# A gated state-space block rewritten: one-pass products on stacked parts, two norms side by side, silus in fours, sums on GpSimd

## The reference

```python
xn = layernorm(x) * norm_w + norm_b
p = xn @ w_in.T;  x1, x2 = p[:C], p[C:]
u = x1 @ ssm_in_w.T
xss, z = silu(u[:C]), silu(u[C:])
xd = einsum(xss, x_proj_w)             # per direction: dtr (R), B (S), C (S)
dt = softplus(einsum(dtr, dt_w) + dt_b)
bc = sum(B * C over S)
y = xss * sum over directions (bc * dt + Ds)
y = (layernorm(y) * out_norm_w + out_norm_b) * z
x = x + ((y @ ssm_out_w.T) * silu(x2)) @ w_out.T
```

## Time and profile before

| | us |
|---|---|
| median of 3 runs (lowest, highest) | 5749.59 (5741.32, 5757.34) |
| span of the profiled execution | 5743.1 |
| the gated block in it: first DMA issue to last write of X | 0.75 to 702.80 |
| first product on x | 35.63 |

### The profile page before, as it was taken

One profiled execution on the slowest core, in us unless ns is written; L12 is line 12 of the kernel. 1 busy time (PEld: TensorE's weight loads), 2 busy tenths in 40 slices (PEclk: granted clock), 3 DMA queues, 4 the chain that ended last, 5 costly groups with the idle time before them and its releaser, 6 DMA issues. The chain is left out here.

```text
span 5743.1 us, 74310 instructions
## 1 busy us (share of the span) xinstructions
PE 4971.3 (87%) x16018; PEld 2207.8 (38%) x16018; DVE 4640.4 (81%) x5047; ACT 2949.7 (51%) x4576; POOL 3832.2 (67%) x2568
## 2 busy tenths in 40 slices
PE   6999889897779999998297888888888888888887
PEld 1222256464256666665152222222222222222222
DVE  4876643434418989899797999999999999999996
ACT  5776544443311111111135777777777777777776
POOL 0000032322418898888786999989998999999993
PEclk9998899998889999998698999999999999999998
DMA  2000000001777787776405667667766666677663
GB/s 47 0 0 0 7 1 1 0 1 56 226 158 139 138 152 140 147 141 107 91 9 138 185 183 189 185 182 189 187 186 178 186 185 187 184 189 189 187 184 100
DMA packets 373418, 711.24 MB, mean 124 GB/s; under 512 B 76604, under 2 KB 111224, under 8 KB 358936
## 3 DMA queue, kind: packets, MB, share of 16 engines
q1 hardware_dynamic: 373144, 708.17, 50.2%
HBM read 575.33 MB, written 82.32 MB: 115 GB/s over the span
## 5 line engine op out<-in xcount | busy, mean ns | idle before, releaser
L2015 POOL TENSOR_TENSOR l_hc<-l_h,l_c_rep 128x512 f32<-128x512 f32 x1536 | 1929.8, 1276 | 216.0 <-DVE l_h L2069 187.1
L2069 DVE TENSOR_TENSOR_SCAN l_h<-l_p_da,l_h,l_bu 128x512 f32<-128x512 f32 x1120 | 1412.8, 1279 | 10.5 <-ACT l_p_da L1920 8.8
L1920 ACT ACTIVATE l_p_da<-l_p_da,l_a_neg 128x512 f32<-128x512 f32 x1536 | 1008.5, 658 | 733.8 <-PE l_p_da L1775 712.9
L1221 POOL TENSOR_TENSOR l2b_prod<-l2b_v,l2b_attn 128x1568 f32<-128x1568 f32 x276 | 937.3, 3461 | 242.9 <-DVE l2b_osum L1269 125.2
L1775 PE MATMUL l_p_da<-l_stacked,l_pick 96*128 96x512 f32 x1536 | 908.9, 593 | 191.3 <-DVE l_h L2069 179.1
L2054 DVE TENSOR_TENSOR l_bu<-l_du_rep,l_p_b 128x512 f32<-128x512 f32 x1280 | 855.7, 669 | 29.7 <-DMA l_du_rep<-du_scratch 22.5
L1775 PEld LDWEIGHTS l_p_da<-l_stacked,l_pick 96*128 96x128 f32 x1536 | 293.7, 192 | 1162.4 <-DVE l_h L2069 900.3
L1269 DVE TENSOR_REDUCE l2b_osum<-l2b_prod 128x32 f32<-128x1568 f32 x384 | 665.7, 1780 | 62.9 <-POOL l2b_prod L1221 59.2
L1783 PE MATMUL l_p_y<-l_hc,l_y_pick 128*32 128x512 f32 x3072 | 566.4, 626 | 74.3 <-POOL l_hc L2015 71.7
L1174 ACT ACTIVATE l2b_logits<-l2b_conv,l2b_this_b 98x512 f32<-98x512 f32 x96 | 66.2, 689 | 870.5 <-PE l2b_conv L1139 870.5
L615 POOL TENSOR_TENSOR l_w_pos_low<-l1a_w_sed,l_w_pos_high 96x1536 fp32r<-96x1536 f32 x1 | 4.1, 4123 | 711.2 <-DVE l_w_fc_high L595 711.2
(11 more groups left out here) (267 smaller groups left out, 8905.2 us busy)
## 6 DMA issues: line engine op xcount, KB each, us to landing
l_du_rep<-du_scratch SPq DMA_DIRECT2D x1536, 256.0 KB, 3.8
l2b_img_high<-qkv_scratch SPq DMA_DIRECT2D x192, 306.2 KB, 5.6
l2b_img_low<-qkv_scratch SPq DMA_DIRECT2D x192, 306.2 KB, 9.4
l_stacked<-l_parts SPq DMA_DIRECT2D x512, 96.0 KB, 2.7
l2b_v<-v_scratch SPq DMA_DIRECT2D x192, 152.0 KB, 6.4
qkv_scratch<-l2a_strip SPq DMA_DIRECT2D x32, 840.0 KB, 5.2
du_scratch<-l_du SPq DMA_DIRECT2D x128, 192.0 KB, 2.1
v_scratch<-l2a_v_strip SPq DMA_DIRECT2D x32, 228.0 KB, 4.2
```

The source lines that it names most:

```text
L1221: return eng.tensor_tensor(dst.rearrange("q x (dy dx) -> q x dy dx", dx=WIN), window, attn_half[:, :, unit % 2].rearrange("q x (dy dx) -> ...
L1920: act.activation(p_da[i % DAS][:], p_da[i % DAS][:], ACT.Exp, scale=a_neg[:, k * G + GRP[i]:k * G + GRP[i] + 1]).then_inc(s_da, 1)
L2015: pool.tensor_tensor(hc[:, (G * par + i) % HCS, :], h[:, i, :], c_rep[:, par, :], ALU.mult).then_inc(s_hc, 1)
L2069: dve.tensor_tensor_scan(h[:, i, way], p_da[i % DAS][:, way], of, state, ALU.mult, ALU.add).then_inc(s_h, 1)
```

## The change

The gated block is rewritten; the other blocks are the same.

- Part of the products becomes one-pass. The weights are no longer multiplied together: one product with `w_bcd` (128 columns) gives the rank parts of all directions twice, b and c. ScalarE copies the two rank parts rounded to float32r, VectorE writes what the rounding left (`rank_low`), and the stack of 96 rows, high, high and low, is the operand of four products with a `w_dt` whose rows are stacked as well (high, low, high). For b*c the stack is high, low and zero rows (`bc_high`, `bc_low`), against `pick`.
- The first norm of tile t+6 and the second norm of tile t-2 lie side by side in two neighbouring banks, and square, Ln, Exp and the product with the inverse deviation work on 1024 elements, where both parts exist.
- The projections and silus of four tiles are taken together, before step t where t is 4g-2 (`project`, `silus`). Tiles are kept in eight slots instead of four. The first centering behind such a group waits for all its silus (`centered`).
- abs is taken from PSUM with the bias on ScalarE, max(.,0) with the bias on VectorE; GpSimd adds the two (`add_log`), adds the directions (`add_gains`, `whole_sum`) and applies the scale and shift of both norms (`affine`).
- The loop is written out, TensorE waits for one quarter of x at a time, and the DMAs are as many as before; the weights of delta and pick are larger (96 x 384 each).

```diff
@@ gated_ssm_block @@
+    GROUP, SLOTS = 4, 8
+    KR, KS = K * R, K * S
...
-        w_bc = sb("l0_w_bc", [C, 2, K * S])
-        xp_dt = sb("l0_xp_dt", [R, K, C])
-        dt_w = sb("l0_dt_w", [R, K, C])
-        w_dt = sb("l0_w_dt", [C, K, C])
-        pick = sb("l0_pick", [K * S, K, C])
+        w_bcd = sb("l0_w_bcd", [C, 128])
+        w_dt = sb("l0_w_dt", [3 * KR, K, C], F32R)
+        pick = sb("l0_pick", [3 * KS, K, C], F32R)
...
+        a = sb("l0_a", [C, SLOTS, N])
+        z = sb("l0_z", [C, SLOTS, N])
+        sg = sb("l0_sg", [C, SLOTS, N])
+        sq = sb("l0_sq", [C, 2, N])
+        rstd = sb("l0_rstd", [C, 2, N])
+        nrm = sb("l0_nrm", [C, 2, N])
+        yz = sb("l0_yz", [C, N])
+        sgated = sb("l0_sgated", [C, N])
+        split = sb("l0_split", [3 * KR, 2, N], F32R)
+        bs = sb("l0_bs", [128, N])
+        bcp = sb("l0_bcp", [KS, N])
+        bc_split = sb("l0_bc_split", [3 * KS, 2, N], F32R)
+        log_part = sb("l0_log_part", [C, K, N])
...
+        half_sum = sb("l0_half_sum", [C, 2, N])
+        whole_sum = sb("l0_whole_sum", [C, 2, N])
...
+        banks = ctx.enter_context(nc.psum_tensor("l0_p", [128, 8, N], F32))
+        p_c, p_v = banks[0:C, 0:2, :], banks[0:C, 2:4, :]
+        p_s, p_o = banks[0:C, 2, :], banks[0:C, 3, :]
+        p_in = [[banks[0:C, i, :] for i in which] for which in ((0, 1, 2), (3, 4, 5))]
+        p_dt = [banks[0:C, 4 + i, :] for i in range(2)]
+        p_bcd, p_bc = banks[:, 6, :], banks[0:C, 7, :]
...
+        def parts_of(n):
+
+            return slice(0 if n >= SLOTS else 1, 2 if n < TILES else 1)
+
+        def all_steps(step, silu_group):
+
+            for t in range(-2, TILES + 2):
+                if t % GROUP == GROUP - 2 and t + 2 < TILES:
+                    silu_group((t + 2) // GROUP)
+                step(t, t >= 0 and t < TILES, t + 1 >= 0 and t + 1 < TILES, t + 2 < TILES, t >= 2)
...
+            def centered(n):
+                if n >= GROUP and n % GROUP == 0 and n <= TILES:
+                    pe.wait_ge(s_silu, n)
+                elif n:
+                    pe.wait_ge(s_nrm, n)
+                if n >= SLOTS:
+                    pe.wait_ge(s_y, n - SLOTS + 1)
+                    mm = pe.matmul(p_c[:, 0, :], center[:], a[:, n % SLOTS, :], start=True, stop=True)
+                if n < TILES:
+                    pe.wait_ge(s_x[n // (TILES // B)], 16)
+                    mm = pe.matmul(p_c[:, 1, :], center[:], X[:, tile(n)], start=True, stop=True)
+                mm.then_inc(s_c, 1)
...
+            def project(g):
+                for j in range(GROUP):
+                    m = GROUP * g + j
+                    pe.wait_ge(s_xn, m + 1)
+                    if j == 0:
+                        pe.wait_ge(s_nrm, m + GROUP)
+                        if g > 1:
+                            pe.wait_ge(s_sgd, m - GROUP)
+                    elif j == 1 and g:
+                        if g > 1:
+                            pe.wait_ge(s_out, GROUP * g - GROUP)
+                        pe.wait_ge(s_mx, K * (GROUP * g - 1))
+                    elif j >= 2:
+                        pe.wait_ge(s_silu, m - 1)
+                    for out, weight in zip(p_in[j % 2], (w_u[:, C:2 * C], w_g[:], w_u[:, 0:C])):
+                        pe.matmul(out, weight, a[:, m % SLOTS, :], start=True, stop=True).then_inc(s_in, 1)
...
+                pe.matmul(p_dt[k % 2], w_dt[:, k, :], split[:, m % 2, :], start=True, stop=True).then_inc(s_dtm, 1)
...
+                pe.matmul(p_bc, pick[:, k, :], bc_split[:, m % 2, :], start=True, stop=True).then_inc(s_bcm, 1)
...
+            def step(t, of_t, of_next, of_second, gated):
+                centered(t + 6)
+                if of_t:
+                    bc_mm(t, 0)
+                if of_next:
+                    dt_mm(t + 1, 0)
+                    dt_mm(t + 1, 1)
+                if of_t:
+                    bc_mm(t, 1)
+                variance(t + 6)
+                if of_next:
+                    dt_mm(t + 1, 2)
+                    dt_mm(t + 1, 3)
+                if of_t:
+                    bc_mm(t, 2)
+                if gated:
+                    s_mm(t - 2)
+                if of_second:
+                    bcd(t + 2)
+                if of_t:
+                    bc_mm(t, 3)
+                if gated:
+                    o_mm(t - 2)
+
+            for n in range(GROUP):
+                centered(n)
+                variance(n)
+            all_steps(step, project)
...
+            def silus(g):
+                for j in range(GROUP):
+                    m = GROUP * g + j
+                    p_z, p_g, p_u = p_in[j % 2]
...
+                    act.activation(z[:, m % SLOTS, :], p_z, ACT.Silu).then_inc(s_z, 1)
...
+                    act.activation(sg[:, m % SLOTS, :], p_g, ACT.Silu).then_inc(s_z, 1)
...
+                    act.activation(a[:, m % SLOTS, :], p_u, ACT.Silu).then_inc(s_silu, 1)
+                act.preload_act_table_set(LN_EXP)
...
+                act.activation(log_part[:, k, :], p_dt[k % 2], ACT.Abs, bias=cols[:, 4 + k:5 + k]).then_inc(s_abs, 1)
...
+            def step(t, of_t, of_next, of_second, gated):
+                square(t + 6)
+                if of_next:
+                    dt_abs(t + 1, 0)
+                    dt_abs(t + 1, 1)
+                    dt_exp(t + 1, 0)
+                inverse_std(t + 6)
+                if of_next:
+                    dt_abs(t + 1, 2)
+                    dt_abs(t + 1, 3)
+                    dt_log(t + 1, 0)
+                    dt_exp(t + 1, 1)
+                    dt_log(t + 1, 1)
+                if of_second:
+                    rank_high_and_b(t + 2)
...
+            def normalise(n):
+                part = parts_of(n)
+                dve.wait_ge(s_rstd, n + 1)
+                if n:
+                    dve.wait_ge(s_xn, min(n, TILES))
+                if n > SLOTS:
+                    dve.wait_ge(s_ya, n - SLOTS)
+                dve.tensor_tensor(nrm[:, part], p_c[:, part], rstd[:, part], ALU.mult).then_inc(s_nrm, 1)
...
+                dve.tensor_tensor(yz[:], yz[:], z[:, m % SLOTS, :], ALU.mult).then_inc(s_yz, 1)
...
+                dve.tensor_tensor(split[2 * KR:3 * KR, m % 2, :], p_bcd[0:KR], split[0:KR, m % 2, :],
+                                  ALU.subtract).then_inc(s_lo, 1)
...
+                dve.tensor_copy(bc_split[0:KS, m % 2, :], bcp[:]).then_inc(s_bhi, 1)
...
+                dve.tensor_tensor(bc_split[KS:2 * KS, m % 2, :], bcp[:], bc_split[0:KS, m % 2, :], ALU.subtract).then_inc(s_blo, 1)
...
+                dve.tensor_scalar(dt[:, m % 2, k, :], p_dt[k % 2], cols[:, 4 + k:5 + k], 0.0, ALU.add, ALU.max).then_inc(s_mx, 1)
...
+                dve.tensor_tensor(gain[:, k, :], p_bc, dt[:, m % 2, k, :], ALU.mult).then_inc(s_gain, 1)
...
+                dve.scalar_tensor_tensor(a[:, m % SLOTS, :], whole_sum[:, m % 2, :], d_sum[:], a[:, m % SLOTS, :],
+                                         ALU.add, ALU.mult).then_inc(s_y, 1)
...
+            def step(t, of_t, of_next, of_second, gated):
+                if of_t:
+                    gains(t, 0)
+                if of_next:
+                    bc_high(t + 1)
+                if of_t:
+                    gains(t, 1)
+                if of_next:
+                    relu(t + 1, 0)
+                    bc_low(t + 1)
+                    relu(t + 1, 1)
+                normalise(t + 6)
+                if of_next:
+                    relu(t + 1, 2)
+                    relu(t + 1, 3)
+                if of_t:
+                    gains(t, 2)
+                if t >= 1 and t <= TILES:
+                    y_of(t - 1)
+                if gated:
+                    times_z(t - 2)
+                if of_t:
+                    gains(t, 3)
+                if gated:
+                    gate(t - 2)
+                if of_second:
+                    rank_low(t + 2)
+                    bc_product(t + 2)
+                if gated:
+                    write_x(t - 2)
...
+            def affine(n):
...
+                if n < TILES:
+                    pool.tensor_scalar(a[:, n % SLOTS, :], nrm[:, 1, :], cols[:, 0:1], cols[:, 1:2],
+                                       ALU.mult, ALU.add).then_inc(s_xn, 1)
+                if n >= SLOTS:
...
+                    pool.tensor_scalar(yz[:], nrm[:, 0, :], cols[:, 2:3], cols[:, 3:4], ALU.mult, ALU.add).then_inc(s_ya, 1)
+
+            def add_log(m, half):
...
+                of = dt[:, m % 2, 2 * half:2 * half + 2, :]
+                pool.tensor_tensor(of, of, log_part[:, 2 * half:2 * half + 2, :], ALU.add).then_inc(s_dt, 1)
+
+            def add_gains(m, part):
...
+                pool.tensor_tensor(half_sum[:, part, :], gain[:, 2 * part, :], gain[:, 2 * part + 1, :],
+                                   ALU.add).then_inc(s_sum, 1)
+
+            def step(t, of_t, of_next, of_second, gated):
+                if of_t:
+                    add_gains(t, 0)
+                affine(t + 6)
```

(21 more changed lines are left out.)

416 lines of the change are left out of this document (151 added, 265 removed).

## The result

The changed kernel takes 5920.64 us (median of 4 runs, 5913.31 to 5922.45), the kernel before 5745.45 us beside it (5737.87 to 5757.34). The ratio is 1.0305, 95% interval 1.0288 to 1.0321: slower by 3%. The profiled execution took 5921.81 us, with a span of 5920.0.

The account below looks back on a forecast made before the run. TensorE bounds the old stage; the new step is one chain through all engines. Start 94, full steps 516, projections 75, light steps 105 and last two 30 end the stage at 820 us; kernel 5867 us, range 5715 to 5955.

Parts of the forecast that it names:

- Start: Beginning of the gated stage: first load at about 14 us, four norms 7.0 us each, first full step at 94 us.
- Full steps: Gated stage: 24 steps of 21.5 us, 516 us; the chain is 17.1 us at full clock, the rest low clock.
- y at 0.74 us in VectorE's chain: VectorE part of the step's chain: y counted at 0.74 us, within 3.6 us for relus, gain, y and times_z.
- the port rival: Two-SBUF-input VectorE operations stall beside GpSimd's half-0 log sum: +2.2 us a step, 5922 us; chance 0.26.
- The clock: TensorE returns low for 4 to 7 us of work after each pause: +2.2, +1.35 and +0.85 us a step.
- Projections: Projections and silus of four tiles as their own block: seven of 12 us, less 9 for warm products, 75 us.
- What was to be seen: Signs: ys 21 us apart, 33 across projections; clock 0.6 to 0.85; TensorE's longest wait for times_z; stage end near 820.
- Light steps: End of the gated stage: six steps without an x part at 17.5 us, 105 us; two last ones 30 us.
- GpSimd's affines: Two one-input scale-and-shift operations a tile on GpSimd, taken at 1.27 us each, beside VectorE's part of the chain.
- Count of products: TensorE before the change: 17 float32 products a tile at 0.86 us, 14.6 us at full clock.
- full clock kept: Rival: TensorE stays at full clock, 24 steps of 17.1 us, stage end 682, kernel 5729 us; chance 0.27.
- the low level would hold throughout: Rival: TensorE stays at the low clock, 24 steps of 24.6 us, stage end 950, kernel 5997 us; chance 0.09.

Follow-up runs that it names:

- Run 3: Changed kernel plus four idle four-pass products on TensorE in each full step, ahead of the scan's output product: 5827.8 us, ratio 1.0146.
- run 1: Changed kernel with y of the tile before made ahead of the normalisation on VectorE, instead of behind the third gain product: 5885.7 us, ratio 1.0248.
- run 2: Changed kernel with GpSimd's first-half sum of the logarithms moved behind the sums of the gains, no longer ahead of y: 5860.5 us, ratio 1.0206.
- run 4: Changed kernel with the eight delta and B times C products of a tile back in four-pass float32: 5972.9 us, ratio 1.0398.
- run 6: Changed kernel with y ahead of normalisation, first log sum behind the gains' sums, and two TensorE products ahead of the scan's output product: 5755.9 us, ratio 1.0010.
- the best version: Kernel of run 9 plus two idle four-pass products ahead of the scan's output product: 5666.2 us, ratio 0.9859.
- run 7: Kernel of run 6 plus four idle four-pass products in the pause ahead of the scan's output product: 5804.9 us, ratio 1.0089.
- run 8: Kernel of run 7 with output product behind the next centerings (except before projections), and direction 2's B times C and gain products ahead of normalisation: 5766.7 us.
- run 9: Kernel of run 8 without idle products, GpSimd's first log sum right behind the product with z instead of behind the gains' sums: 5718.3 us, ratio 0.9949.

## Why the prediction was right, and what it missed

The side was right, and so was the reason: the engines that did the work have less of it, and the period is a chain. The range (5715 to 5955) holds 5920.6. The forecast of 5867 was 54 us low, and part of its nearness is luck: the stage itself is 68 us longer than forecast (887.8 against 820), and the later stages and the difference of median and span, which have nothing to do with the argument, give 14 back. By its own steps:

- **Start**: the first product on x at 16.07 us (14 forecast); the first full step would begin at 96.4 us without its projection, 94 forecast. The four norms are 7.0 us apart, as worked out.
- **Full steps**: those within a group last 23.7 us on average, 21.5 forecast: 53 us in 24 steps, most of the 68. Run 3 has steps of 18.3 us in which every product is full and y is stretched, so the 23.7 are a chain of 16.4 at the full level (17.1 forecast), 1.9 for y (nothing forecast) and 5.4 for the low level (4.4 forecast). The term that was mis-sized most is **y at 0.74 us in VectorE's chain**. It lasts 2.65 beside the log sum, 1.91 more a step, or 46 us. It is the port rival as it was written (2.2 us a step, on GpSimd's sum for half 0); that its 5922 us lie so near the 5920.6 measured is luck again, since its other terms are those of the forecast. Runs 1 and 2 show the cause: the stretch goes over to the operation that stands beside the sum, and it goes away when the sum moves. I had kept this rival out of the forecast because the profile before showed only casts stalled; no row spoke for two-input operations, and none against. The rule of the Trainium skill ("SBUF — State Buffer", section "Who interferes with whom") that two-SBUF-input operations of VectorE and a GpSimd operation that reads SBUF exclude each other is borne out by y, by the product with z and by `bc_low` (1248 ns beside GpSimd's half sum; in the full steps this is slack, as VectorE still waits ahead of the normalisation, 2.32 us in the timeline above); the gate, with one input from PSUM, is not touched.
- **The clock**: the total of 4.4 us a step is near the 5.4, but its parts offset each other. The engine stays low for longer than the 4 to 7 us of work that were worked out from the QKV stage: behind the pause at 595 us the products are low until 606.5 us, some 10 us of work. The output product and the centerings, taken low in half of the steps, are low in all and in three of four; the variances, taken low in one of three at 2.6 us, are low in one of four and cost 1.8 (24.9 against 23.1 us).
- **Projections**: each takes 13.4 to 13.6 us on TensorE, from its first product to the centering behind it, 12 forecast; as the centerings behind it are full, the seven add 80 us to steps of 23.7, 75 forecast.
- **What was to be seen**: ys 21 us apart and 33 across a projection (23 to 25 and 34.8), the clock between 0.6 and 0.85 (0.65 in the stage, but 0.50 in some stretches of 20 us), and TensorE's wait for the product with z its longest (7.7 us, 185 in all).
- **Light steps** (the six without a part of x): 19.2 us instead of 17.5, 10 us in all. y is stretched in them too (2.62 us), but run 2, which takes that away, shows steps of 20.1 instead of 20.5, so what they cost is not shown to be the port's. The last two take 27 instead of 30.
- **Around the stage**: the later stages are 8 us shorter and the median lies 0.6 us above the span instead of 6.5.
- **GpSimd's affines**, taken at 1.27 us, take 0.77 and 0.78. They are hidden themselves, but the size was not without effect: GpSimd's sum of the logarithms starts as the second affine ends (591.90 us), when its own input has been ready for 0.7 us, and so they set where the sum stands against y, 0.24 us ahead of it. What longer ones would have done no run shows.
- **Count of products**: the kernel before makes 18 products a tile, not 17 (two centerings, two variances, three projections, b and c, four for delta, four for b*c, s and o; its 1152 records are 32 times 36). At 0.86 us that is 15.5 us and not 14.6. The chain does not use this number. The new kernel issues eleven weight loads where the kernel before issued twelve.
- **Rivals**: "full clock kept" would have been the fast side. Run 3 shows what it needs: work in TensorE's pauses. Without it the clock does not stay full here. The loss is not that of the one-pass products, which gave 52 us (run 4). That the low level would hold throughout was near in some stretches (0.50) but not on average.

What ended the gain, then: the change cut the work of TensorE, VectorE and ScalarE but made TensorE's written order pass through VectorE, GpSimd and ScalarE once a tile. Moving members off that path gave 165 us (run 6), overlapping the output product and refitting the log sum another 38, and holding the clock up 52 more. Since a move changes the level too, and the level changes which wait ends last, these amounts hold for the order in which the moves were made. That the projection's block could overlap the steps was not tried; in the best version a write of X across it is still 27.3 us behind the last one, where a step takes 13.7. Nor were four idle products tried together with the refitted log sum, so what part of their loss in runs 7 and 8 is their own stays open.

## What to carry to other kernels

Before you trade TensorE's work for the work of others, write down the chain of one step from the last instruction back to itself. If no engine is busy for most of that length, what decides is which instructions stand in the written order between two members of the chain, and moving one changes the time without changing the work. Lay GpSimd's long SBUF operations beside VectorE operations that read PSUM, and look at every pause of some microseconds that the new chain gives TensorE in each step, because the products that follow it may be paid at the low level (here behind pauses of 3.2 us and more, in nearly all steps not behind 1.5). After each move look for the next member: the late log sum held up no full step in run 6 and three of four in run 7.

## What the runs showed of the hardware

- Work that nobody reads can pay: four four-pass products of 0.86 us in a pause of 7.4 us raised the granted clock from 0.64 to 0.87 and took 93 us off the kernel. In the chain of 15 to 17 us of run 9, two gave 52 us and three the same. Four on top of run 6 went with a loss of 49 us, in part because they began at the low level, took 6.47 us and held up the products behind them, in part because of the late log sum. A filler pays while the level stays full and is in the way when it begins low: with three, the full steps ran at 13.7 us throughout and the last ones at 17.
- A VectorE operation with both inputs in SBUF, begun 0.24 us behind a GpSimd sum of 2.35 us, lasts 2.65 us instead of 0.74. Moving it hands the stretch to the next two-input operation (2.41 us on average instead of 0.68), and only 35 us were gained, where moving the sum gave 60. A cast from SBUF to SBUF is hit too (1.90 us instead of 0.41, beside the log sums of run 7). Who starts first is spared: a cast begun 0.01 us ahead of the sum took 0.41 us, and the sum 2.64 instead of 2.35.
- GpSimd's one-input multiply and add on 96x512 takes 0.77 us, its two-input sum 1.27 (2.35 on 96x1024).
